# One-hot rows of the second edge loop made by ScalarE instead of by VectorE comparisons

## The reference

```
e0, e1 = feat0[edge_src], feat1[edge_src]          # gathered rows of 32 + 96 numbers
ea0, ea1 = edge_attr[:, :1], edge_attr[:, 1:4]
h = gelu(edge_scalar_attr @ W_mlp1 / sqrt(8))
h = gelu(h @ W_mlp2 / sqrt(64))
w00, w01, w10, w11 = h @ Wp_00, h @ Wp_01, h @ Wp_10, h @ Wp_11
out0_a = w00 * e0 * ea0
out0_b = w11 * sum(e1 * ea1[:, None, :], -1) / sqrt(3)
out1_a = (w01 * e0)[:, :, None] * ea1[:, None, :]
out1_b = w10[:, :, None] * e1 * ea0[:, :, None]
n0, n1 = segment_sum(mid0, edge_dst), segment_sum(mid1, edge_dst)
```

## Time and profile before

| | us |
|---|---|
| median of three runs | 5571.94 |
| profiled execution | 5537.74 |
| its span | 5536.0 |
| PE busy, share of the span | 3748.7 (68%) |
| POOL busy | 3393.7 (61%) |
| DVE busy | 3229.4 (58%) |
| ACT busy | 1795.8 (32%) |

### The profile page before, as it was taken

The page is one execution under the profiler, slowest core; times in us unless marked ns, Lnnn a source line. Parts: engine busy times, 40 slices in busy tenths (PEclk is TensorE's granted clock), DMA queues, the critical chain, the costliest instruction groups (busy, mean ns, idle before and its releaser), DMA issues. The chain is left out here.

```text
span 5536.0 us, 64081 instructions
## 1 busy us (share of the span) xinstructions
PE 3748.7 (68%) x14998; PEld 2529.6 (46%) x14998; DVE 3229.4 (58%) x10179; ACT 1795.8 (32%) x5061; POOL 3393.7 (61%) x3252
## 2 busy tenths in 40 slices
PE   2566666667676766776747777677677676775865
PEld 2244444444444444444435555455454554554644
DVE  3344555555555555555546666566676675664856
ACT  1244444444444444444432222122222221221221
POOL 4455555555555555555447776667676767766764
PEclk6787888888888888888867888778787887887877
DMA  5343443434443434444311111111111111111111
GB/s 173 108 114 101 112 113 108 112 108 106 112 110 105 113 108 114 112 112 112 84 50 43 42 43 42 45 44 44 42 43 44 43 40 46 43 41 44 44 43 54
DMA packets 322951, 431.52 MB, mean 78 GB/s; under 512 B 127443, under 2 KB 212647, under 8 KB 322440
## 3 DMA queue, kind: packets, MB, share of 16 engines
q0 software_dynamic: 103168, 211.49, 14.7%
q1 hardware_dynamic: 219256, 215.77, 13.9%
q10 hardware_dynamic: 144, 0.05, 0.0%
HBM read 410.36 MB, written 16.65 MB: 77 GB/s over the span
## 5 line engine op out<-in xcount | busy, mean ns | idle before, releaser
L219 POOL DMA_INDIRECT ahead_rows<-feat,c_src_tiles x1612 | 1827.1, 1133 | 815.6 <-issue 493.4
L181 POOL DMA_INDIRECT ring_rows<-xl,c_src_tiles x1612 | 1534.9, 952 | 1178.5 <-DVE attn_msg L1092 647.8
L932 PE MATMUL attn_sums_ps<-attn_msg,attn_onehot 128*128 128x136 f32 x3224 | 551.0, 324 | 726.9 <-DVE c_acc_attn L1033 526.1
L1585 PE MATMUL conv_sums_ps<-conv_vals,conv_onehot 128*128 128x256 f32 x3224 | 914.3, 433 | 108.2 <-issue 57.3
L1623 ACT ACTIVATE conv_scaled<-conv_w_ps,c_xT 128x64 f32<-128x64 f32 x1612 | 373.5, 314 | 1758.0 <-remote 807.0
L1592 PE MATMUL conv_w_ps<-c_Wp,conv_hid 128*128 128x256 f32 x1612 | 491.1, 433 | 618.9 <-ACT conv_hid L1629 345.1
L932 PEld LDWEIGHTS attn_sums_ps<-attn_msg,attn_onehot 128*128 128x128 f32 x3224 | 483.6, 223 | 781.6 <-issue 769.6
L1585 PEld LDWEIGHTS conv_sums_ps<-conv_vals,conv_onehot 128*128 128x128 f32 x3224 | 650.2, 212 | 338.7 <-issue 165.2
L981 ACT ACTIVATE attn_fifth<-attn_pre_ps,c_b_r 128x512 f32<-128x512 f32 x403 | 275.4, 683 | 1349.8 <-remote 779.8
L1098 DVE SCALAR_TENSOR_TENSOR attn_leaky<-attn_pre_ps,c_b_r,attn_fifth 128x512 f32<-128x512 f32 x403 | 301.3, 748 | 704.1 <-ACT attn_fifth L981 455.4
L1648 DVE TENSOR_SCALAR conv_onehot<-c_iota,c_dst_pos 128x128 f32<-128x128 f32 x1612 | 355.3, 297 | 608.0 <-remote 525.6
(11 more groups left out here) (221 smaller groups left out, 4685.4 us busy)
## 6 DMA issues: line engine op xcount, KB each, us to landing
c_xT<-in_attrT SPq DMA_DIRECT2D x403, 256.0 KB
attn_rel<-rel_group SPq DMA_DIRECT2D x403, 126.0 KB
ring_rows<-xl,c_src_tiles POOLq DMA_INDIRECT x1612
ahead_rows<-feat,c_src_tiles POOLq DMA_INDIRECT x1612
attn_xr_win<-xr_parts SPq DMA_DIRECT2D x403, 31.5 KB
ahead_radial<-in_radial_halves SPq DMA_DIRECT2D x101, 64.0 KB
attn_limit<-limit SPq DMA_DIRECT2D x403, 16.0 KB
xr_parts<-set_parts SPq DMA_DIRECT2D x13, 384.0 KB
```

The costliest lines, as they stand in the source:

```text
L181: pool.indirect_dma_start(self.rows[:, b, t, :], None, self.q["xl"][:, :], bass.IndirectOffsetOnAxis(ap=self.idx[:, bass.ds(k.index(TG, t) ...
L219: pool.indirect_dma_start(self.rows[:, k.slot(U), t, :], None, self.q["feat"][:, :], bass.IndirectOffsetOnAxis(ap=self.idx[:, bass.ds(k.in ...
L932: last = nc.tensor.matmul(to, onehot[:, g.slot(2), t, :], msg[:, g.slot(2), t, :, :].rearrange("p h o -> p (h o)"), start=wins > 1 or t == ...
L1585: last = nc.tensor.matmul(to, onehot[:, g.slot(2), t, :], vals[:, g.slot(2), t, :], start=wins > 1 or t == 0, stop=wins > 1 or t == TG - 1)
```

## The change

The four comparisons leave DVE's step. ACT's step gets, as its last part, four Abs activations (each 128x128) and one Relu activation over 128x512, which works in place on the one-hot buffer. Between them stands a wait for a new semaphore `far_ready`, since the Relu reads what the four before it wrote. The wait for the sums of group k-5, which frees the buffer, moves with them. Nothing else is changed; the one-hot rows hold the same numbers.

```diff
+        far_ready = sem("far_ready")
@@ def _(act): def body(k, live):  (after the gelu of group k)
+                if live(3):
+                    g = k.back(3)
+                    at_least(act, sums_ready, g.back(2).uses())
+                    for t in range(TG):
+                        nc.scalar.activation(onehot[:, g.slot(2), t, :], sb["iota"][:, :], ACT.Abs, bias=sb["dst_pos"][:, bass.ds(g.index(TG, t), 1)], scale=-1.0).then_inc(far_ready, 1)
+                    act.wait_ge(far_ready, g.uses(1, TG))
+                    nc.scalar.activation(onehot[:, g.slot(2), :, :], onehot[:, g.slot(2), :, :], ACT.Relu, bias=sb["one"][:, :], scale=-1.0).then_inc(onehot_ready, 1)
@@ def _(dve): def body(k, live):
-                    if live(3):
-                        g = k.back(3)
-                        at_least(dve, sums_ready, g.back(2).uses())
-                        for t in range(TG):
-                            last = nc.vector.tensor_scalar(onehot[:, g.slot(2), t, :], sb["iota"][:, :], sb["dst_pos"][:, bass.ds(g.index(TG, t), 1)], None, ALU.is_equal)
-                        last.then_inc(onehot_ready, 1)
```

## The result

The changed kernel takes 6190.96 us (median of 4 runs, 6156.90 to 6203.92) and the kernel before 5567.56 us on the same chip: a ratio of 1.114, 95% interval 1.109 to 1.118. It is 623 us slower; 225 us had been forecast, and 6191 us lies above the range that ended at 6150.

The account below looks back on a forecast made before the run. Waits, with no engine fully busy, were taken to pace the second loop at 6.54 us a step. 402 x (7.1 - 6.54) = 225 us slower, added to 5537.74 us plus 34 us, gave about 5800 us, range 5640 to 6150.

Parts of the forecast that it names:

- The place: Second loop: activations behind ACT's last gelu make PE wait 2.41 us before each step's sums; full-clock round 6.32 us.
- What DVE gains: Second loop: without four comparisons DVE's round falls from 3.98 to 3.1 us, worth 0.14 us in an undisturbed step.
- undisturbed step: Second-loop step without late results: PE's round is 3.84 us, DVE's 3.98 us, so DVE is slower by a hair.
- What goes away: Second loop: at 6.32 us or more a step POOL rests after four gathers, so late results become rare, under 200 us.
- Late results: PE's results reaching ACT late in the second loop while POOL gathers without pause; 764.3 us and 90.2 us of waits.
- The closing of node batches: Second loop: this work falls into PE's and DVE's new idle time and costs nothing more.
- The clock: Second loop: PE's waits bring half clock part of the time; mean 0.86 makes 6.32 us a step 7.07, taken as 7.1.
- share of 0.76: Second loop: at half clock PE works 7.7 of a 10.1 us round, and half of that share is lost.
- A: Rival, second loop: the clock stays full, 6.32 us a step, about 5485 us, faster; chance 0.08.
- B: Rival, second loop: gathers set the pace, some 6.4 us for four, so nothing changes, 5572 us; chance 0.03.
- C: Rival, second loop: late results keep their total, 2.2 us a step on top of 6.32, some 6360 us; chance 0.04.
- D: Rival, second loop: half clock for good, a round of 10.1 us, about 7000 us; chance 0.04.

Follow-up runs that it names:

- e1: Changed kernel with the same five activations moved to the head of ACT's step, ahead of the scaling; 5540 us, 0.996 of the kernel before.
- e3: Changed kernel with the four Abs at the head of ACT's step and only the Relu last; 5663 us, 1.017 of the kernel before.
- e12: Changed kernel with a second Relu over the same rows behind the first, changing nothing in them; 6434 us, 1.139 of the kernel before.
- e4: Second loop with one-hot rows set to zero once and made by no engine; 5533 us, 0.994 of the kernel before.
- e5 to e7: Unread matmuls before PE's sums: four in e1, four in the kernel before, three in e1; 1.017, 1.017 and 1.019 of the kernel before.
- e2: Changed kernel with four unread matmuls a step in PE's wait before the sums; 5576 us, 1.001 of the kernel before.
- e11: Changed kernel with two unread matmuls a step in PE's wait before the sums; 5749 us, 1.018 of the kernel before.
- e10: Changed kernel with two of the four gathers a step left out from step 11 on; 6249 us, 1.105 of the kernel before.
- e9: Kernel before with two of the four gathers a step left out from step 11 on; 4682 us, 0.829 of the kernel before.

## Why the prediction was wrong

*The place, right.* The wait was 2.42 us a step for 2.41, ended by the Relu, and the rounds with the least low clock take 6.35 us for 6.32. e1 shows that it comes from the place alone, e3 and e12 that it follows what stands last.

*What DVE gains, right in size.* It was put at 0.14 us in an undisturbed step and nothing in the others: e4 gains 0.6%, some 34 us or 0.09 us a step. In which steps it gains them isn't shown, and since the gathers set the kernel's average, the reason given (PE is next) isn't what e4 tested.

*What goes away, right in its outcome.* Late results vanished and POOL came to rest. The reading behind it, that rests end them, didn't hold: e5 to e7 have rests and late results both. Late results are rare or missing in every kernel whose own round is 6.4 us or more (e2, e11, the changed one, e12), and there by the hundred microseconds in every one with four gathers and a shorter round. That the changed kernel's 6.35 us and more are slow enough for the gathers fits this; it was right by luck. The closing of node batches cost nothing more, as predicted: but for the first, no round is over 9.6 us.

*The clock, wrong in size, and this is the step that failed.* The prediction took a mean of 0.86, "near the first loop's, whose gaps are the likest", and let the half clock fall on PE's work with a share of 0.76. Measured is a mean of 0.76. The share follows from it: a full-clock round is 6.32 us and the mean 8.10, so the low clock cost 1.78 us a step, which is half of 3.56 us of work at half clock; the half clock lasted 2 x (1 - 0.76) x 8.10 = 3.89 us. So 0.91 of it lay on work. The trace gives the same directly: 0.92 of the time at half clock lies on instructions of PE. By the prediction's own formula, a clock of 0.76 gives 6.32 / (1 - 0.48 x 0.76 x 0.5) = 7.73 us and a share of 0.91 then 8.09. Of the missing 1.0 us a step, 0.63 is the mean clock and 0.37 the place where the low clock falls. The windows above show the second in two of three rounds: the clock was 1.00 while PE rested and 0.56 and 0.69 while it worked. The share of 0.76 was the share of work in a round run wholly at half clock; it took for granted that the two are independent, and they aren't. That the cost hangs on the clock is shown by e2: with ACT's chain unchanged and the clock held at 0.99, the time is that of the kernel before (1.001). Why the mean fell to 0.76 and not to 0.86 stays open; the first loop, from which 0.86 was taken, has other waits.

*The range.* Its upper end used 0.72 with the wrong share, or 6150 us. The pair of 0.76 and 0.91 gives 5763 + 402 x 0.99 + 34 = 6195 us, which only says that the account adds up, since both were taken from the result.

*The rivals.* A (full clock, 5485 us) didn't occur, and e2, where the clock was held up, shows that its price was a little low: 5576 us and 6.56 us a step, of which the usual round, 6.39 us, comes close to A's 6.32, and the 30 longer rounds are the rest. B (the gathers set the pace) had 0.03. For the changed kernel it is false (e10), for the kernel before it is true (e9), and the argument against it, that "in undisturbed steps the ring feeds 3.98 us", was weak: the ring can do that for some steps, not on the average. The chance of 0.03 was far too low for a mechanism that does hold in the kernel it was read from. C (late results on top, 6360 us) came nearer in time than the forecast, by accident: the late results that it adds are gone. D (7000 us) was far off.

*The page of the Trainium skill.* "TensorE: Matmul & The Clock Gate", section "HAM oscillation — how this bites in real kernels", spoke against the change: bursts with waits between begin cold. The trace agrees with it in part: of three rounds, each begun after a wait of 2.4 us, those of 9.19 and 8.03 us began at the half clock, and the one of 6.34 us did its work at 1.00.

## What to carry to other kernels

Work moved to an idle engine costs what its place in that engine's order costs: ahead of the step's waits the five activations were free (0.996), behind the last gelu they cost 11%. When a change puts a wait into each round of TensorE, reckon with the low clock on the work and not evenly on the round, look at how long the wait is (1.2 us cost no clock in e3's undisturbed rounds, 2.4 us took it to 0.76), and test it by filling the wait with unread matmuls. Before a gain is promised from a lighter engine, leave out half of each other resource in turn: here half the gathers gave 17%, and all one-hot work gave 0.6%.

## What the runs showed of the hardware that was not expected

- The clock can be full in most of the rests and at half for most of the work: with a wait of 2.4 us a round, 61% of PE's busy time and 14% of its rests were at the half clock, over some 400 rounds.
- Its mean doesn't fall steadily with the rest: waits of 1.45, 2.4 and 3.1 us a round gave 0.94, 0.76 and 0.80 (e11, changed, e12), and 1.17 us gave 1.00 in e3's undisturbed rounds. Why is open; PE's work in the round isn't the same in e11.
- 1612 indirect gathers of 128 rows kept to 6.5 to 6.85 us for four on the average in all kernels whose own round was 5.6 us or less, though one takes 0.94 us and the next follows 0.30 us later, and though the DMA engines were busy 17% of the time. When they are pushed beyond it, results of PE reach ACT and DVE late. With two gathers a step nothing of this is left. What sets this pace wasn't found.
- The releaser that a profile names can be the wrong engine: L1688 of DVE was named in 364 steps, while in all 403 groups ACT's Relu ended later than the values that the sums needed.
